# A layer norm's reciprocal root moved from ScalarE's Ln and Exp to VectorE's bit trick and three Newton steps

## The chip, the cores and the metric

One core of one Trainium2 chip runs the whole program in one launch. The metric is device time in microseconds (us), lower is better. The comparison is between the kernel before and the kernel with the change, on the same chip.

## The reference, cut to what matters

The model is one graph layer followed by one mixture-of-experts layer over 12,500 nodes of 256 features and 200,000 edges. Only the front of the graph layer is touched:

```python
def _layernorm(x, axis=-1, eps=1e-05):
    m = jnp.mean(x, axis=axis, keepdims=True)
    v = jnp.var(x, axis=axis, keepdims=True)
    return (x - m) / jnp.sqrt(v + eps)

ft = (feat @ W).reshape(n, H, OUT)            # feat = _layernorm(x), 4 heads of 64
e_src = jnp.sum(ft * w_att_src, axis=-1)      # per node and head
e_dst = jnp.sum(ft * w_att_dst, axis=-1)
e = leaky_relu(e_src[src] + e_dst[dst])       # per edge, softmax over the edges of dst
out = segment_sum(ft[src] * a, dst)           # then x + out, layer norm, experts
```

## The kernel before, in words

The program is a row of stages, each of which is a block that all engines enter and leave together: constants, edge rows, edge tables, **features**, a look-up table of scores, the main stage over the edges, and the experts. The change is in `features` (L720 to L874) and in the two helpers that it calls, `layer_norm_steps` (L92) and `rsqrt_guess` (L121). The main stage calls `rsqrt_guess` too (L1238), for its own layer norm, and that call stays.

`features` works on 98 tiles of 128 nodes, in 14 batches of HB = 7 tiles. Batches alternate between two halves of every buffer (h = 0 for even batches, 1 for odd). For one batch:

- SyncE loads 7 tiles of x in one transfer (L747) and stores 7 rows of results to the table in memory (L754). Its queue is in order. One turn of its loop waits until the even batch's norm is done, loads the next even batch, does the same for the odd batch, and then waits for ScalarE's rows and stores the even batch and the odd batch. So the load of the next even batch stands behind the store of the odd batch before.
- VectorE takes 7 statistics (L98), 7 aggregations (L102), adds epsilon (L104), and then asks ScalarE for a guess of the reciprocal root: `dve.wait_ge(ln_given, nth)`. One Newton step of four small operations follows (L106 to L112), and 7 normalising operations of 128x256 (L117). Those wait until TensorE is through with the batch that used the same buffer before.
- ScalarE computes that guess as Exp(-0.5 * Ln(v)) (L125, L127). In its program the guess for batch q + 1 stands in the middle of batch q, at tile u = 2, after the copy for tile 3 and ahead of the rows of tile 2. Its other work for every tile is a copy of the transposed tile from PSUM (L809), a copy of the result row of 264 values (L822) and of 8 scores (L823).
- TensorE transposes a tile (L844) and multiplies it with the weights (L860); it transposes tile u + 1 ahead of multiplying tile u. The multiplication of tile u waits for ScalarE's copy of u, and for ScalarE's rows of tile u - 2, since there are two result banks.

Each step is ordered by semaphores written out by hand; `Steps.did` and `Steps.settle` put a semaphore wait between any two dependent VectorE operations. At the stage's last batches SyncE's queue is special: the last load has a short tile, for which it waits until VectorE has cleared the buffer after norm 12, and the stores of batches 10 and 11 stand behind that.

Of the kernel before, what the change touches and what calls it, by code (L numbers as in the profile page):

```python
# [7 lines left out]
I32 = mybir.dt.int32  # L8
ALU = mybir.AluOpType
# [4 lines left out]
P = 128  # L14
# [34 lines left out]
HB = 7  # L49
# [4 lines left out]
EPS = 1e-5  # L54
# [9 lines left out]
RSQRT_BITS = float(0x5f3759df)  # L64
# [24 lines left out]
        self.engine.wait_ge(self.sem, self.base + self.n)  # L89

def layer_norm_steps(nc, st, raw, stats, mv, rs, normed, n, ln_asked, ln_given, nth, free=None):  # L92

    dve = nc.vector
    v, r, t = rs
    for i in range(n):
        st.did(dve.bn_stats(stats[:, i, :], raw[:, i, :]))  # L98
    st.settle()
    st.did(dve.memset(t[:, 0:n], 0.0))  # L100
    for i in range(n):
        st.did(dve.bn_aggr(mv[:, i, :], stats[:, i, :]))  # L102
    st.settle()
    dve.tensor_scalar(v[:, 0:n], mv[:, 0:n, 1], EPS, None, ALU.add).then_inc(ln_asked, 1)  # L104
    dve.wait_ge(ln_given, nth)
    st.did(dve.tensor_tensor(t[:, 0:n], r[:, 0:n], r[:, 0:n], ALU.mult))  # L106
    st.settle()
    st.did(dve.tensor_tensor(t[:, 0:n], t[:, 0:n], v[:, 0:n], ALU.mult))
    st.settle()
    st.did(dve.tensor_scalar(t[:, 0:n], t[:, 0:n], -0.5, 1.5, ALU.mult, ALU.add))  # L110
    st.settle()
    st.did(dve.tensor_tensor(t[:, 0:n], t[:, 0:n], r[:, 0:n], ALU.mult))  # L112
    if free is not None:
        dve.wait_ge(*free)
    st.settle()
    for i in range(n):
        st.did(dve.tensor_scalar(normed[:, i, :], raw[:, i, :], mv[:, i, 0:1], t[:, i:i + 1],  # L117
                                 ALU.subtract, ALU.mult))

def rsqrt_guess(nc, n, v, r, asked, given, between, nth):  # L121

    act = nc.scalar
    act.wait_ge(asked, nth)
    act.activation(r[:, 0:n], v[:, 0:n], ACT.Ln).then_inc(between, 1)  # L125
    act.wait_ge(between, nth)
    act.activation(r[:, 0:n], r[:, 0:n], ACT.Exp, scale=-0.5).then_inc(given, 1)  # L127
# [589 lines left out]
def features(nc, x, K, table):  # L717
# [3 lines left out]
    with ExitStack() as ctx:  # L721
        sb = lambda n, s, d=F32: ctx.enter_context(nc.sbuf_tensor("f_" + n, s, d))
        xin = [sb(f"xin{h}", [P, HB, D]) for h in range(2)]
        xn = [sb(f"xn{h}", [P, HB, D]) for h in range(2)]
        rowbuf = [sb(f"rowbuf{h}", [P, HB, ROW]) for h in range(2)]
        xT = [sb(f"xT{i}", [P, 2 * P]) for i in range(2)]
        stats, mv = sb("stats", [P, HB, 6]), sb("mv", [P, HB, 2])
        rs = (sb("v", [P, HB]), sb("r", [P, HB]), sb("t", [P, HB]))
        psT = [ctx.enter_context(nc.psum_tensor(f"f_T{i}", [P, 512], F32)) for i in range(2)]
        psF = [ctx.enter_context(nc.psum_tensor(f"f_F{i}", [P, 512], F32)) for i in range(2)]  # L730
        names = ("padded", "steps", "asked", "given", "between", "normed", "turned", "copied",
                 "multiplied", "row_made", "scored")
        padded, steps, asked, given, between, normed, turned, copied, multiplied, row_made, scored = [
            ctx.enter_context(nc.semaphore("f_" + n)) for n in names]
        loaded = [ctx.enter_context(nc.semaphore(f"f_loaded{h}")) for h in range(2)]
        stored = [ctx.enter_context(nc.semaphore(f"f_stored{h}")) for h in range(2)]
        block = ctx.enter_context(nc.Block("features"))
        LAST = NQ // 2 - 1
        STEPS = 3 * HB + 5

        def rows_of(t, q, n=HB):
            return t[bass.ds(q * (HB * P), n * P), :].rearrange("(b p) d -> p b d", p=P)
# [1 line left out]
        @block.sync  # L744
        def _(sp):
            def load(q, h):
                sp.dma_start(xin[h][:, :, :], rows_of(x, q)).then_inc(loaded[h], 16)  # L747

            def freed(h, it):
                sp.wait_ge(normed, 2 * it + h + 1)  # L750

            def store(q, h, it):
                sp.wait_ge(row_made, (2 * it + h + 1) * HB)
                sp.dma_start(rows_of(table, q), rowbuf[h][:, :, :]).then_inc(stored[h], 16)  # L754

            def iteration(it, more):
                freed(0, it)
                load(2 * it + 2, 0)
                freed(1, it)
                if more:  # L760
                    load(2 * it + 3, 1)
                else:

                    sp.dma_start(xin[1][:, 0:HB - 1, :], rows_of(x, NQ - 1, HB - 1)).then_inc(loaded[1], 16)
                    sp.wait_ge(padded, 1)
                    sp.dma_start(xin[1][0:LASTROWS, HB - 1, :], x[(NB - 1) * P:N, :]).then_inc(loaded[1], 16)
                store(2 * it, 0, it)
                store(2 * it + 1, 1, it)

            load(0, 0)  # L770
            load(1, 1)
            with sp.Fori(0, LAST - 1) as it:
                iteration(it, True)
            iteration(LAST - 1, False)
            store(2 * LAST, 0, LAST)
            store(2 * LAST + 1, 1, LAST)
            for h in range(2):
                sp.wait_ge(stored[h], 16 * (LAST + 1))

        @block.vector  # L780
        def _(dve):
            def norm(q, h, it, first=False, extra=0):
                st = Steps(dve, steps, q * STEPS)
                dve.wait_ge(loaded[h], 16 * (it + 1) + extra)

                layer_norm_steps(nc, st, xin[h], stats, mv, rs, xn[h], HB, asked, given, q + 1,
                                 None if first else (multiplied, (q - 1) * HB))
                st.settle()
                dve.nop().then_inc(normed, 1)
                assert st.n == STEPS  # L790

            nc.vector.memset(K.scores[:, NB:NBD, :], 0.0)
            norm(0, 0, 0, first=True)
            norm(1, 1, 0, first=True)
            with dve.Fori(1, LAST) as it:
                norm(2 * it, 0, it)
                norm(2 * it + 1, 1, it)
            norm(2 * LAST, 0, LAST)
            dve.wait_ge(normed, 2 * LAST)
            nc.vector.memset(xin[1][64:P, HB - 1, :], 0.0).then_inc(padded, 1)  # L800
            norm(2 * LAST + 1, 1, LAST, extra=16)

        @block.scalar
        def _(act):
            def make_rows(q, h, it, more=True):
                def copy_turned(u):
                    k = (h * HB + u) % 2
                    act.wait_ge(turned, q * HB + u + 1)
                    nc.scalar.activation(xT[k][:, :], psT[k][:, 0:2 * P], ACT.Copy).then_inc(copied, 1)  # L809

                copy_turned(0)
                for u in range(HB):
                    i = q * HB + u
                    k = (h * HB + u) % 2
                    if u + 1 < HB:
                        copy_turned(u + 1)
                    if u == 2 and more:
                        rsqrt(q + 1)
                    if u == 0 and it is not None:
                        act.wait_ge(stored[h], 16 * it)  # L820
                    act.wait_ge(multiplied, i + 1)
                    nc.scalar.activation(rowbuf[h][:, u, :], psF[k][:, 0:ROW], ACT.Copy).then_inc(row_made, 1)  # L822
                    nc.scalar.activation(K.scores[:, bass.ds(i, 1), :].rearrange("p a b -> p (a b)"),  # L823
                                         psF[k][:, MSG:NF], ACT.Copy).then_inc(scored, 1)

            rsqrt = lambda q: rsqrt_guess(nc, HB, rs[0], rs[1], asked, given, between, q + 1)
            rsqrt(0)
            make_rows(0, 0, None)
            make_rows(1, 1, None)
            with act.Fori(1, LAST) as it:  # L830
                make_rows(2 * it, 0, it)
                make_rows(2 * it + 1, 1, it)
            make_rows(2 * LAST, 0, LAST)
            make_rows(2 * LAST + 1, 1, LAST, more=False)

        @block.tensor
        def _(pe):
# [1102 lines left out]
```

## Time and profile before

| | us |
|---|---|
| median of 3 runs | 3243.91 (3243.89 to 3252.16) |
| the profiled execution | 3247.97 |
| its span in the profile | 3246.2 |
| mean granted TensorE clock | 0.863 |
| PE, DVE, ACT, POOL busy | 2351.3, 1787.3, 1503.8, 2189.2 |
| feature stage, first x load to last table store's issue | 81.3 to 261 |

The span is the time between the first and the last recorded instruction; the execution's own time has 1.8 us around it. Times of rows count from the span's start. The busy sums cover all stages together, while stages follow one another, so they don't tell what bounds the feature stage; windows and timelines of that stage do.

### The profile page before, as it was taken

The numbers are of one execution on the slowest core, as the hardware profiler recorded it, in microseconds if no ns is written. First come the engines' busy times: TensorE is split into PE (matmuls) and PEld (weight loads), VectorE is DVE, ScalarE is ACT, GpSimd is POOL, SyncE is SP. The second block draws the span as 40 slices with busy tenths as digits, with TensorE's granted clock in tenths as the row PEclk, the third lists the DMA queues.
The fourth block names the chain that finished last, engine by engine and source line by source line (L and its number), as shares of the span: only waits on it lengthen the run. The fifth ranks groups of instructions, "written<-read, shape, count | busy, mean of one in ns | idle before, by whom it ended". The sixth has DMA issues, their size and how long they took to land. (4 is left out here: it accounts for less than half of the span.)

```text
span 3246.2 us, 61769 instructions
## 1 busy us (share of the span) xinstructions
PE 2351.3 (72%) x15568; PEld 1904.9 (59%) x15569; DVE 1787.3 (55%) x3822; ACT 1503.8 (46%) x2731; POOL 2189.2 (67%) x2064
## 2 busy tenths in 40 slices
PE   2673666667667677667777777777767999898995
PEld 1552545555555555556565666666646787777774
DVE  4453444445555556667677777777769433332232
ACT  0562222333344444445555565666654554444442
POOL 0004777777777777777777777777614777777775
PEclk9996777778787777888888888899888999999997
DMA  3444555555555555566666566656524355545443
GB/s 96 146 147 134 155 156 155 157 162 164 165 165 164 166 166 168 167 175 178 173 185 181 173 187 177 182 176 186 164 78 63 62 79 81 81 78 80 80 79 47
DMA packets 232170, 452.82 MB, mean 139 GB/s; under 512 B 55832, under 2 KB 148796, under 8 KB 230783
## 3 DMA queue, kind: packets, MB, share of 16 engines
q0 software_dynamic: 114816, 265.53, 35.2%
q1 hardware_dynamic: 76924, 142.54, 13.7%
q10 hardware_dynamic: 39924, 38.86, 3.7%
q8 instruction: 213, 3.49, 0.4%
q14 instruction: 293, 2.40, 0.2%
HBM read 379.15 MB, written 69.01 MB: 138 GB/s over the span
## 5 line engine op out<-in xcount | busy, mean ns | idle before, releaser
L977 POOL DMA_INDIRECT m_rows<-table,src_col x1568 | 1600.1, 1020 | 729.3 <-issue 700.1
L1363 PE MATMUL m_A<-m_msg,m_by_edge 128*128 128x260 f32 x3920 | 1176.3, 463 | 259.0 <-issue 207.4
L1363 PEld LDWEIGHTS m_A<-m_msg,m_by_edge 128*128 128x128 f32 x3920 | 895.9, 235 | 451.9 <-issue 270.3
L1217 ACT ACTIVATE m_apart<-m_drow,nid 128x1024 bf16 x297 | 341.0, 1148 | 726.2 <-SPq L945 684.9
L1053 DVE TENSOR_TENSOR m_msg<-m_rows,m_A 128x2048 f32<-128x2048 f32 (+1 forms) x294 | 568.2, 1932 | 115.1 <-issue 109.3
L1349 PE MATMUL m_E<-m_look_parts,m_by_node 128*128 x7104 | 246.9, 168 | 259.4 <-ACT m_by_node L1220 258.7
L1349 PEld LDWEIGHTS m_E<-m_look_parts,m_by_node 128*128 128x128 bf16 x7104 | 232.8, 98 | 343.7 <-issue 307.4
L1571 POOL DMA_INDIRECT out<-x_con,x_to_i x206 | 329.2, 1598 | 105.0 <-issue 78.7
L1029 DVE TENSOR_TENSOR m_z<-m_E,m_rows 128x64 f32<-128x64 f32 x295 | 65.9, 224 | 566.9 <-PE m_E L1349 435.7
L1220 ACT ACTIVATE m_by_node<-m_apart,m_one 128x1024 bf16<-128x1024 bf16 x297 | 340.9, 1148 | 9.7
L1013 DVE SCALAR_TENSOR_TENSOR m_by_edge<-dst_col,m_less_base,row 128x1024 f32<-128x1024 f32 (+1 forms) x295 | 325.3, 1103 | 0.7 <-issue 0.2
L1738 DVE TENSOR_TENSOR x_con<-x_X,x_b 128x512 f32<-128x512 f32 x103 | 71.2, 692 | 391.3 <-DMA out<-x_con,x_to_i 358.9
L1562 POOL DMA_INDIRECT x_yr<-ydram,x_from_i x206 | 204.9, 995 | 65.9 <-issue 62.1
L1797 ACT ACTIVATE x_h<-x_H,x_b 128x256 f32<-128x256 f32 x206 | 86.4, 470 | 298.0 <-PE x_H L1852 298.0
L1852 PE MATMUL x_H<-x_yT,x_c 128*128 128x256 f32 x824 | 201.6, 388 | 13.7 <-issue 11.4
L1225 ACT ACTIVATE m_z<-m_z 128x32 f32<-128x32 f32 x295 | 67.3, 228 | 302.7 <-issue 157.5
L1863 PE MATMUL x_X<-x_c,x_h 128*128 128x256 f32 x824 | 195.5, 381 | 2.8 <-DVEq L1745 2.8
L1852 PE MATMUL x_G<-x_h,x_c 128*128 128x256 f32 x824 | 194.7, 379 | 0.0
L1787 ACT ACTIVATE x_c<-x_w 128x512 f32 x309 | 182.7, 627 | 6.0 <-DVEq L1719 5.1
L1852 PEld LDWEIGHTS x_H<-x_yT,x_c 128*128 128x128 f32 x824 | 149.6, 191 | 44.7 <-issue 28.5
L1863 PEld LDWEIGHTS x_X<-x_c,x_h 128*128 128x128 f32 x824 | 157.1, 191 | 24.2 <-issue 3.2
L1852 PEld LDWEIGHTS x_G<-x_h,x_c 128*128 128x128 f32 x824 | 156.9, 190 | 20.9
(245 smaller groups left out, 2232.3 us busy)
## 6 DMA issues: line engine op xcount, KB each, us to landing
m_drow<-edges SPq DMA_DIRECT2D x196, 512.0 KB
m_rows<-table,src_col POOLq DMA_INDIRECT x1568
table<-f_rowbuf SPq DMA_DIRECT2D x14, 924.0 KB, 5.0
ydram<-m_y ACTq DMA_DIRECT2D x49, 264.0 KB
m_xb<-in_x ACTq DMA_DIRECT2D x48, 256.0 KB
out<-m_x ACTq DMA_DIRECT2D x48, 256.0 KB
f_xin<-in_x SPq DMA_DIRECT2D x13, 896.0 KB, 6.5
x_w<-in_L_ffn_expert_w SPq DMA_DIRECT2D x18, 256.0 KB, 5.7
```

The source lines that it names most:

```text
L977: nc.gpsimd.indirect_dma_start(rows[:, g % RING, j, :], None, table, bass.IndirectOffsetOnAxis(ap=K.src_col[:, g, j:j + 1], axis=0)).then_ ...
L1013: v.scalar_tensor_tensor(by_edge[q][:, tiles, :], K.dst_col[:, bass.ds(group, 1), tiles].rearrange("p a j -> p (a j)").unsqueeze(2).broadc ...
L1053: v.tensor_tensor(msg[i][:, tiles, 0:D].rearrange("p j (h n) -> p j h n", h=HEADS), rws[:, tiles, 0:D].rearrange("p j (h n) -> p j h n", h ...
L1217: a.activation(apart[i][:, :], drow[:, bass.ds(g % RING, 1), :].rearrange("p a n -> p (a n)"), ACT.Abs, bias=K.nid[:, bass.ds(b, 1)], scal ...
L1220: a.activation(by_node[i][:, :], apart[i][:, :], ACT.Relu, bias=one[:, 0:1], scale=-1.0)\
L1349: m = t.matmul(psE[i][:, 8 * j:8 * j + 8], by_node[i][:, j * P:(j + 1) * P], look_parts[:, bass.ds(b, 1), 8 * n:8 * n + 8].rearrange("p a ...
L1363: m = t.matmul(psA[i][:, 0:MSG], by_edge[i][:, j, :], msg[i][:, j, :], start=(j == tiles[0]), stop=(j == tiles[-1]))
L1562: g.indirect_dma_start(yr[t % YR][:, i, :], None, ydram, bass.IndirectOffsetOnAxis(ap=from_i[:, 2 * t + i:2 * t + i + 1], axis=0))\
L1571: g.indirect_dma_start(out, bass.IndirectOffsetOnAxis(ap=to_i[:, 2 * t + i:2 * t + i + 1], axis=0), con[t % CR][:, i, :], None, bounds_che ...
L1787: a.activation(into[t % 2][:, :, :].rearrange("p c n -> p (c n)"), of[:, bass.ds(expert(t), 1), :, :].rearrange("p e c n -> p (e c n)"), A ...
L1852: i = t_.matmul(ps[t % 2][:, m * TILE:(m + 1) * TILE], weight[t % 2][:, c, m * P:(m + 1) * P], of[t % 2][:, c, :], start=(c == 0), stop=(c ...
L1863: m = t_.matmul(psX[t % 2][:, i * D:(i + 1) * D], h2[t % 2][:, c, i * P:(i + 1) * P], c3[t % 2][:, c, :], start=(c == 0), stop=(c == 1))
```

## The change

In `layer_norm_steps` the request to ScalarE and the wait for it go. VectorE adds epsilon, shifts the variance's bits right by one as an integer (`arith_shift_right`), computes RSQRT_BITS minus that as the bits of the first guess, and runs three Newton steps of three operations. The normalising operations read the root from `r` and not from `t`. In `features` ScalarE's program no longer holds the guess: it has only its copies. The main stage is as it was.

```diff
-def layer_norm_steps(nc, st, raw, stats, mv, rs, normed, n, ln_asked, ln_given, nth, free=None):
+def layer_norm_steps(nc, st, raw, stats, mv, rs, normed, n, free=None):
...
-    dve.tensor_scalar(v[:, 0:n], mv[:, 0:n, 1], EPS, None, ALU.add).then_inc(ln_asked, 1)
-    dve.wait_ge(ln_given, nth)
-    st.did(dve.tensor_tensor(t[:, 0:n], r[:, 0:n], r[:, 0:n], ALU.mult))
+    st.did(dve.tensor_scalar(v[:, 0:n], mv[:, 0:n, 1], EPS, None, ALU.add))
     st.settle()
-    st.did(dve.tensor_tensor(t[:, 0:n], t[:, 0:n], v[:, 0:n], ALU.mult))
+    st.did(dve.tensor_scalar(half_bits[:, 0:n], v[:, 0:n].bitcast(I32), 1, None, ALU.arith_shift_right))
     st.settle()
-    st.did(dve.tensor_scalar(t[:, 0:n], t[:, 0:n], -0.5, 1.5, ALU.mult, ALU.add))
-    st.settle()
-    st.did(dve.tensor_tensor(t[:, 0:n], t[:, 0:n], r[:, 0:n], ALU.mult))
+    st.did(dve.tensor_scalar(r[:, 0:n].bitcast(I32), half_bits[:, 0:n], -1.0, RSQRT_BITS, ALU.mult, ALU.add))
+    for _ in range(3):
+        st.settle()
+        st.did(dve.tensor_tensor(t[:, 0:n], r[:, 0:n], r[:, 0:n], ALU.mult))
+        st.settle()
+        st.did(dve.scalar_tensor_tensor(t[:, 0:n], t[:, 0:n], -0.5, v[:, 0:n], ALU.mult, ALU.mult))
+        st.settle()
+        st.did(dve.scalar_tensor_tensor(r[:, 0:n], t[:, 0:n], 1.5, r[:, 0:n], ALU.add, ALU.mult))
...
-                    if u == 2 and more:
-                        rsqrt(q + 1)
...
-            rsqrt = lambda q: rsqrt_guess(nc, HB, rs[0], rs[1], asked, given, between, q + 1)
-            rsqrt(0)
```

## Rows read from the trace of the kernel before

**Rows 1.** Windows, one per feature batch: us, busy by engine, PEclk, DMA.
```profile
95.69:108.28 12.59, 10.53 (x42) 8.05 (x43) 6.34 (x28) 7.73 (x23) 0.00 (x0) 1.00 0.22 74
108.28:120.77 12.49, 10.09 (x44) 7.79 (x42) 7.98 (x34) 7.90 (x25) 0.00 (x0) 0.86 0.50 150
120.77:131.74 10.97, 8.37 (x44) 6.58 (x42) 4.11 (x22) 7.91 (x25) 0.00 (x0) 1.00 0.54 170
131.74:144.54 12.80, 10.05 (x44) 7.64 (x42) 8.20 (x34) 7.90 (x25) 0.00 (x0) 0.87 0.50 147
...
155.62:168.19 12.57, 9.93 (x43) 7.60 (x42) 8.07 (x33) 7.90 (x25) 0.00 (x0) 0.87 0.47 148
...
190.30:203.04 12.74, 10.05 (x43) 7.75 (x42) 7.47 (x33) 8.07 (x25) 0.00 (x0) 0.87 0.50 151
...
214.04:226.78 12.74, 10.05 (x44) 7.86 (x43) 7.68 (x33) 8.07 (x25) 0.00 (x0) 0.87 0.52 157
226.78:237.78 11.00, 8.37 (x44) 6.58 (x43) 4.46 (x23) 7.90 (x25) 0.00 (x0) 1.00 0.17 60
237.78:251.38 13.60, 10.03 (x43) 7.58 (x42) 6.20 (x28) 7.80 (x25) 0.00 (x0) 0.87 0.44 146
251.38:260.26 8.88, 8.27 (x43) 6.41 (x41) 0.00 (x0) 5.15 (x21) 0.00 (x0) 1.00 0.31 107
```

**Rows 2.** Timeline, TensorE and ScalarE: start, us, engine, what, [idle before it <-releaser].
```profile
153.81 1.97 PE L860 MATMUL f_F<-wcat,f_xT 128*128 128x268 f32 x8
155.62 0.60 PE L844 MATMUL f_T<-ident,f_xn 128*128 128x128 f32 x4
...
159.90 1.28 ACT L125 ACT_TABLE_LOAD   x1
161.42 1.28 ACT L127 ACT_TABLE_LOAD   x1
162.83 0.37 ACT L822 ACTIVATE f_rowbuf<-f_F 128x264 f32<-128x264 f32 x1
163.59 1.17 PE L860 MATMUL f_F<-wcat,f_xT 128*128 128x268 f32 x4 [2.02 <-ACT f_xT L809]
```

**Rows 3.** Timeline, VectorE in one batch, with the next batch's first operation.
```profile
155.62 2.39 DVE L98 BATCH_NORM_STATS2 f_stats<-f_xin 128x6 f32<-128x256 f32 x7 [0.51 <-DVE f_xn L117]
158.66 0.17 DVE L104 TENSOR_SCALAR f_v<-f_mv 128x7 f32<-128x7 f32 x1
162.96 0.17 DVE L106 TENSOR_TENSOR f_t<-f_r 128x7 f32<-128x7 f32 x1 [4.13 <-ACT f_r L127]
163.76 2.35 DVE L117 TENSOR_SCALAR f_xn<-f_xin,f_mv,f_t 128x256 f32<-128x256 f32 x7
166.26 2.39 DVE L98 BATCH_NORM_STATS2 f_stats<-f_xin 128x6 f32<-128x256 f32 x7
```

**Rows 4.** Groups of instructions by line and shape, other stages: busy us, mean ns.
```profile
L1113 DVE SCALAR_TENSOR_TENSOR m_newton<-m_newton,m_var 128x2 f32<-128x2 f32 x49 | 7.9, 162 | 1.7
L1669 DVE TENSOR_SCALAR x_rest_i<-x_rest_i 128x6 int32<-128x6 int32 x1 | 0.2, 171 | 0.0
```

**Rows 5.** Timeline, SyncE's queue and ScalarE's wait at batch 12.
```profile
192.02 0.40 SPq L747 DMA_DIRECT2D f_xin<-in_x  x1
...
243.27 0.39 ACT L822 ACTIVATE f_rowbuf<-f_F 128x264 f32<-128x264 f32 x1 [4.28 <-DMA table<-f_rowbuf]
```

**Rows 6.** The page, transfers: KB each, median us from issue to landing.
```profile
f_xin<-in_x SPq DMA_DIRECT2D x13, 896.0 KB, 6.5
```

**Rows 7.** Timeline, the stage after the features, its first operation.
```profile
265.82 0.85 DVE L634 TENSOR_REDUCE lt_ends<-scores 128x4 f32<-128x392 f32 x1 [14.88 <-PEq L721]
```

**Rows 8.** Groups of ScalarE's instructions by line, whole span.
```profile
L125 ACT ACT_TABLE_LOAD x63 | 80.8, 1283 | 86.4 <-PEq L428 81.2 <-issue 2.5
...
L1228 ACT ACTIVATE m_msg<-m_z 128x32 f32<-128x32 f32 x295 | 67.6, 229 | 9.4
```

**Rows 9.** The page's first line.
```profile
span 3246.2 us, 61769 instructions
```

More of the change, by code:

```diff
@@ L89, in settle @@
         self.engine.wait_ge(self.sem, self.base + self.n)
-def layer_norm_steps(nc, st, raw, stats, mv, rs, normed, n, ln_asked, ln_given, nth, free=None):
+def layer_norm_steps(nc, st, raw, stats, mv, rs, normed, n, free=None):
     dve = nc.vector
-    v, r, t = rs
+    v, r, t, half_bits = rs
     for i in range(n):
@@ L116, in layer_norm_steps @@
     for i in range(n):
-        st.did(dve.tensor_scalar(normed[:, i, :], raw[:, i, :], mv[:, i, 0:1], t[:, i:i + 1],
+        st.did(dve.tensor_scalar(normed[:, i, :], raw[:, i, :], mv[:, i, 0:1], r[:, i:i + 1],
                                  ALU.subtract, ALU.mult))
@@ L727, in features @@
         stats, mv = sb("stats", [P, HB, 6]), sb("mv", [P, HB, 2])
-        rs = (sb("v", [P, HB]), sb("r", [P, HB]), sb("t", [P, HB]))
+        rs = (sb("v", [P, HB]), sb("r", [P, HB]), sb("t", [P, HB]), sb("half_bits", [P, HB], I32))
         psT = [ctx.enter_context(nc.psum_tensor(f"f_T{i}", [P, 512], F32)) for i in range(2)]
         psF = [ctx.enter_context(nc.psum_tensor(f"f_F{i}", [P, 512], F32)) for i in range(2)]
-        names = ("padded", "steps", "asked", "given", "between", "normed", "turned", "copied",
-                 "multiplied", "row_made", "scored")
-        padded, steps, asked, given, between, normed, turned, copied, multiplied, row_made, scored = [
+        names = ("padded", "steps", "normed", "turned", "copied", "multiplied", "row_made", "scored")
+        padded, steps, normed, turned, copied, multiplied, row_made, scored = [
             ctx.enter_context(nc.semaphore("f_" + n)) for n in names]
@@ L738, in features @@
         LAST = NQ // 2 - 1
-        STEPS = 3 * HB + 5
+        STEPS = 3 * HB + 13
         def rows_of(t, q, n=HB):
@@ L784, in norm @@
                 dve.wait_ge(loaded[h], 16 * (it + 1) + extra)
-                layer_norm_steps(nc, st, xin[h], stats, mv, rs, xn[h], HB, asked, given, q + 1,
+                layer_norm_steps(nc, st, xin[h], stats, mv, rs, xn[h], HB,
                                  None if first else (multiplied, (q - 1) * HB))
@@ L804, in _, with make_rows @@
         def _(act):
-            def make_rows(q, h, it, more=True):
+            def make_rows(q, h, it):
                 def copy_turned(u):
@@ L833, in _ @@
             make_rows(2 * LAST, 0, LAST)
-            make_rows(2 * LAST + 1, 1, LAST, more=False)
+            make_rows(2 * LAST + 1, 1, LAST)
         @block.tensor
```

## The prediction

> **What bounds the kernel now.** I read the page first and then left it: its busy sums run over stages that follow one another, and the span of 3246.2 us [rows 9] is worth something here only as the ruler. The question is what sets the length of the feature stage, and whether its end sets the rest. The second is quickly read: the next stage's first operation comes at 265.82, after VectorE has idled for 14.88 us, released by the end of the block [rows 7]. Every microsecond taken off the end of the features moves all later stages up by the same.
>
> The first I read from windows cut at TensorE's first transposition of every batch [rows 1]. The 14 batches take 95.69 to 260.26, 164.57 us, and fall into four kinds. Six take 10.97 to 11.11 at full clock (two of them are shown). Five take 12.49, 12.80, 12.57, 12.74 and 12.74 with a mean granted clock of 0.86 or 0.87. Two are special, batch 0 (12.59) and batch 12 (13.60). The last, batch 13, takes 8.88 to the end of its last matmul. It is the only batch in which ScalarE computes no guess for a next one, so it is a measurement of the stage without what the change removes. To compare it with the others, which are cut where the next transposition starts: that start lies 0.16 us ahead of the end of the matmuls before it (153.81 + 1.97 = 155.78 against 155.62) [rows 2]. So a batch without guess takes 8.88 - 0.16 = 8.72 us, and one with guess 11.00, of which TensorE is busy 8.37.
>
> Where the 2.28 us go stands in the timeline of one batch. ScalarE loads a table at 159.90, another at 161.42, and gets to the rows of tile 2 at 162.83. That is 2.93 us in which it copies nothing, and TensorE's next matmul at 163.59 has idled 2.02 us for ScalarE's copy of a transposed tile [rows 2]. VectorE meanwhile waits 4.13 us for the guess [rows 3], but it is not late: its wait costs nothing as long as the normed tiles come before TensorE ends the batch. So TensorE, held up by ScalarE's in-order program, is the path, with VectorE and the transfers beside it.
>
> **The change part by part.**
>
> *ScalarE's guess goes.* In 13 batches (0 to 12) the gap in ScalarE's program closes. In the eleven ordinary ones and batch 0 the price is 11.00 - 8.72 = 2.28 us each [rows 1]. In batch 12 ScalarE waits 4.28 us for a store at its first row [rows 5], and the guess partly lies beside the catching-up that follows. What that batch can give lies between 0 and 13.60 - 8.72 = 4.88. The store stands behind norm 12 in SyncE's queue, and norm 12 will come somewhat earlier against TensorE, which takes part of the stall away. I take 2.28 here too, near the middle. Sum: 13 x 2.28 = 29.6 us.
>
> *The clock.* Five batches are longer by (12.49 + 12.80 + 12.57 + 12.74 + 12.74) - 5 x 11.00 = 8.3 us together. They show TensorE's granted clock at the lower of its two levels (1.2 of 2.4 GHz) for part of the batch; in finer windows the fall comes each time one or two microseconds after the idle time of 2.02 us. Batch 13, without that idle time, has 1.00 throughout [rows 1]. With the stall gone I expect none of the five falls: 8.3 us, with 0 as the other end if the short gaps at batch borders were enough. I take the whole, since no fall in this stage lies anywhere but behind a stall. Batch 0's excess over 11.00 (1.59) comes from the start, at the lower level, and stays.
>
> *VectorE's chain in batch 0.* Nothing hides the root there: TensorE waits for the first normed tiles. Before, from the epsilon operation on: that operation (0.20 to the next start), then Ln, one table load and Exp, 162.96 - (159.90 + 1.28) = 1.78, then four small operations from 162.96 to 163.76, 0.80 [rows 2, 3], in all 2.78. (Ln's own table load came before the wait.) After: epsilon, shift, subtraction and nine Newton operations, 12 x 0.20 = 2.40. The nearest rows for the new kinds are an int32 TENSOR_SCALAR of 128x6 at 171 ns and a SCALAR_TENSOR_TENSOR of 128x2 at 162 ns [rows 4], no dearer than the 0.17 of the small ones here. Gain 0.4; between 1.0 and a loss of 0.9 if the steps were 0.15 or 0.31 us.
>
> *VectorE's chain elsewhere.* Per batch: statistics and aggregation 158.66 - 155.62 = 3.04, 2.40 for the root, and from the first normalising operation to the next batch's statistics 2.50 (163.76 to 166.26), or 2.86 at a turn of the loop (0.51 of idle time as at 155.62) [rows 3]. That is 7.94 or 8.30, mean 8.12, against TensorE's 8.72. It is hidden, with only 0.60 us per batch to spare; if the cover is gone each 0.05 us on a small operation costs 0.60 us per batch, and from there on 14 x what is over.
>
> *SyncE and the transfers.* Nothing is issued anew, but the same 1.8 MB per batch must pass in 8.72 us instead of 11.0. The DMA share was 0.54 in such batches [rows 1], so 0.54 x 11.0 / 8.72 = 0.68 now. The tight spot is the load of an even batch behind an odd store: it starts at 192.02 where batch T began at 190.30, so at T + 1.72, lands 6.5 later (median [rows 6]), and needs 3.04 + 2.40 + 2.50 on VectorE: T + 16.2. TensorE asks for it two batches after T, at T + 17.4. Slack 1.2 us per pair; hidden, but next in line.
>
> Sum: 29.6 + 8.3 + 0.4 = 38.3 us. The profiled execution of 3247.97 would become 3209.7; it lay 4.06 above the median of the runs, so against that median 3243.91 - 38.3 = 3205.6. As a check: 14 x 8.72 + 1.59 for batch 0 + 2.6 left for batch 12 = 126.3, 164.57 - 126.3 = 38.3.
>
> *The skill against the trace.* The trace has two loads of 1.28 us per guess and ScalarE's next function right behind each [rows 2]. The Trainium skill, "ScalarE: Activation LUTs", section "Table sets: the hidden batching unit", says that Ln and Exp share a set, so that a sequence of both needs one load; if so here, there would be no loads after the first and a guess would hardly stall TensorE. The trace disagrees: 63 loads stand at L125 [rows 8], one per guess, and one more ahead of each Exp [rows 2]. The same page, "What ACT_TABLE_LOAD costs", gives 2.66 us for a switch with its drain; 13 batches would then give an estimated 13 x 2 x (2.66 - 1.28) = 36 us more. The gap of 2.93 us from the first load to the next copy leaves no room for that, and the measurement decides.
>
> **The rivals.**
>
> *A. The clock still falls.* All else as forecast, but the clock falls in as many batches: gain 30.0, 3213.9. For it: short idle times of TensorE remain at each batch border (0.6 us). Against: they are there in batch 13 too, at 1.00.
>
> *B. VectorE or the even load becomes the bound.* The slacks are 0.60 and 1.2/2 us per batch. If small operations step at 0.26 instead of 0.20, VectorE needs 8.84; if the load lands in 9.2 rather than 6.5 because a load, a store and the next load now overlap more, a pair is 1.5 us late. Six pairs x 1.5 = 9 us given back: 3214.6. For it: the chain is really close. Against: bandwidth is there (share 0.68).
>
> *C. Slower: table loads move into the main stage.* ScalarE's Exp for the edges (L1228, 295 times) finds its table without any load: the main stage's loads all stand at L125 and L127. At the stage's entry that rests on the feature stage having ended with Exp's table. Afterwards the features hold only copies. If the placement then puts a load ahead of Exp in every item, that is 295 x 1.283 = 378 us of ScalarE [rows 8], up to 3243.9 - 38.3 + 378 = 3584 if all of it were on the path. The change turns slower once over 38.3 / 1.283 = 30 of the 295 loads are exposed; a quarter exposed gives 3300. Against: the last guess of each pair leaves Exp's table behind, so one load at the entry is enough, 1.3 us at most.
>
> *D. The change doesn't pay:* the shorter features are given back in a later stage, within 10 us of before. Nothing in [rows 7] speaks for it: the next stage waits for the block.
>
> **How the numbers follow.** Forecast 0.66 (3205.6, own range 3200 to 3210), A 0.10, B 0.15, C 0.03, D 0.03, and a gain above 46 us 0.03. The range 3198 to 3217 holds the forecast, A and B and leaves out C, D and the tails. This measurement tells apart changes above 0.3%, 9.7 us. Faster by more takes in the forecast, A, B, the larger gain: 0.94. Within: D, 0.03. Slower: C, 0.03.
>
> **What would show it.** Right: batches 1 to 11 at 8.7 us from transposition to transposition, a granted clock of 1.00 from batch 1 to 11, no idle time of about 2 us ahead of L860, no table load between 96 and 222 us, VectorE idle for short times only, and a stage end near 222 instead of 260; later stages as long as before. Wrong: batches of 9.5 us or more with TensorE's transposition released by the norm (B), falls of the clock (A), more than 50 table loads at the main stage or any ahead of L1228 beyond the first (C), or small VectorE operations that start more than 0.25 us apart.

## The result: 24.7 us faster, 13.6 us less than forecast

The changed kernel takes 3219.31 us (median of 4 runs, 3216.11 to 3222.28), the kernel before 3244.01 us beside it (median of 4, 3243.89 to 3252.16): ratio 0.9918, 95% interval 0.9898 to 0.9937. The sign is as forecast; the size is not: 3205.6 was predicted, with a range of 3198 to 3217. Two more samples of the same kernel, below, gave 26.9 and 23.7 us.

The profiled execution took 3221.51 us, with this first line of the page:

```profile
span 3219.8 us, 61872 instructions
```

The span is 26.4 us shorter than the 3246.2 of [rows 9]. First the features, cut at TensorE's first transposition of each batch as in [rows 1] (us, busy by engine in the order PE, PEld, DVE, ACT, POOL, granted clock, DMA share, GB/s):

```profile
95.01:105.25 10.24, 10.19 (x42) 7.99 (x43) 9.40 (x41) 4.98 (x19) 0.00 (x0) 0.79 0.36 102
105.25:113.77 8.52, 8.13 (x43) 6.54 (x42) 7.82 (x39) 5.16 (x21) 0.00 (x0) 1.00 0.62 205
113.77:122.46 8.69, 8.11 (x44) 6.54 (x42) 5.15 (x27) 5.15 (x21) 0.00 (x0) 1.00 0.83 263
...
148.69:157.54 8.85, 8.11 (x44) 6.55 (x43) 6.54 (x33) 5.26 (x21) 0.00 (x0) 1.00 0.76 233
...
192.57:201.24 8.67, 8.10 (x43) 6.54 (x42) 7.09 (x34) 5.15 (x21) 0.00 (x0) 1.00 0.25 82
201.24:211.32 10.08, 8.36 (x43) 6.57 (x42) 7.31 (x34) 5.05 (x21) 0.00 (x0) 1.00 0.58 196
211.32:220.16 8.84, 8.27 (x43) 6.41 (x41) 0.00 (x0) 5.15 (x21) 0.00 (x0) 1.00 0.31 107
```

Batches 1 to 11 take 8.52 to 8.89 us where they took 10.97 to 12.80, and the granted clock is 1.00 in each. The last batch, which had no guess before either, is as long as it was (8.84 against 8.88). The stage ends at 220.16 instead of 260.26: 40.1 us earlier. So the features gave what was forecast and 1.8 us more.

The timeline of one batch (start, us, engine, line, what, [idle before it <- releaser]) answers to [rows 2] and [rows 3]:

```profile
150.03 1.14 PE L858 MATMUL f_F<-wcat,f_xT 128*128 128x268 f32 x4 [0.74 <-ACT f_xT L811]
150.32 0.17 DVE L104 TENSOR_SCALAR f_v<-f_mv 128x7 f32<-128x7 f32 x1
150.53 0.17 DVE L106 TENSOR_SCALAR f_half_bits<-f_v 128x7 int32<-128x7 int32 x1
150.73 0.17 DVE L108 TENSOR_SCALAR f_r<-f_half_bits 128x7 int32<-128x7 int32 x1
150.94 0.17 DVE L111 TENSOR_TENSOR f_t<-f_r 128x7 f32<-128x7 f32 x1
...
152.74 2.35 DVE L120 TENSOR_SCALAR f_xn<-f_xin,f_mv,f_r 128x256 f32<-128x256 f32 x7
...
156.91 1.41 DVE L98 BATCH_NORM_STATS2 f_stats<-f_xin 128x6 f32<-128x256 f32 x4 [1.82 <-DMA f_xin<-in_x]
```

TensorE's idle time of 2.02 us is gone; the 0.74 at the head of this batch is all that is left. VectorE's twelve small operations start 0.20 us apart (150.32 to 152.74 is 2.42). VectorE waits for the next load six times, 3.1 us at most, which TensorE doesn't feel.

Then the later stages. The first operation of the next stage [rows 7] is still 40.09 us early:

```profile
225.73 0.85 DVE L637 TENSOR_REDUCE lt_ends<-scores 128x4 f32<-128x392 f32 x1 [15.56 <-PEq L724]
```

The main stage is bracketed by its first and last gather, here of the kernel before and of the changed one (ns min/median/max, first and last start):

```profile
L977 POOL DMA_INDIRECT m_rows<-table,src_col x1568: 947/953/2015, 275.6 to 2372.1; - x196
```

```profile
L975 POOL DMA_INDIRECT m_rows<-table,src_col x1568: 951/957/2016, 235.5 to 2336.5; - x196
```

40.1 us ahead at the first gather, 35.6 at the last. The next loss stands in VectorE's timeline of the experts' routing, first before the change, then after it:

```profile
2442.08 0.26 DVE L1635 TENSOR_TENSOR x_g<-x_top 128x98 f32<-128x98 f32 x1
2442.49 0.77 DVE L1597 TENSOR_TENSOR x_eq<-x_pr,x_top 128x588 f32<-128x588 f32 x1
2443.30 0.77 DVE L1599 TENSOR_TENSOR x_eq<-x_eq,x_rev 128x588 f32<-128x588 f32 x1
...
2447.67 0.26 DVE L1648 TENSOR_TENSOR x_g<-x_g 128x98 f32<-128x98 f32 x1
```

```profile
2407.61 0.26 DVE L1633 TENSOR_TENSOR x_g<-x_top 128x98 f32<-128x98 f32 x1
2408.02 0.77 DVE L1595 TENSOR_TENSOR x_eq<-x_pr,x_top 128x588 f32<-128x588 f32 x1
2413.96 0.77 DVE L1597 TENSOR_TENSOR x_eq<-x_eq,x_rev 128x588 f32<-128x588 f32 x1 [5.17 <-issue]
...
2418.34 0.26 DVE L1646 TENSOR_TENSOR x_g<-x_g 128x98 f32<-128x98 f32 x1
```

34.5 us ahead at the first x_g, 29.3 at the second. Between two operations that followed each other at once, VectorE now stands still for 5.17 us, and "issue" says that no semaphore, no engine and no transfer of the kernel's released it. The stage's code is the same in both kernels. The transfers of that stretch (2405 to 2430) show what else was moved: two packets on the queue of instruction fetches, first the changed kernel, then the same stretch of the kernel before, which has none, and where the kernel's own queue has the whole:

```profile
q1 hardware_dynamic: 13558, 3.38, 81.0%
q14 instruction: 2, 0.02, 0.2%
```

```profile
q1 hardware_dynamic: 12757, 3.13, 100.4%
```

The first of the two begins inside the stop: asked in narrow windows, none lies in 2408.8 to 2412.0 and one in 2412.0 to 2412.4. VectorE stops at 2408.79 and goes on at 2413.96, 1.9 us after that packet began.

So 4.5 us in the main stage, 1.1 between it and the routing, 5.1 in the routing and 2.9 in the experts' part are given back, and the gain of 40.1 becomes 26.4. What these have in common, and which of them is more than the difference between one execution and another, is what the experiments ask. What the change leaves behind for the later stages is where their code stands. Compiled, VectorE's program has 3384 instructions against 3328, since the root is written out once for each call of the norm: 56 more ahead of the main stage, and everything later stands 56 places further down. ScalarE's program is 25 instructions shorter (3024 against 3049); the other engines' are as long as before.

### The profile page after: what moved, and what is told of

Same layout as the page of the kernel before. It is cut to its first block and busy times, and to the rows that moved or that the text cites. A ratio compares the mean times of both kernels' runs of the same rounds, so it can differ in the third digit from the quotient of the medians.

```text
span 3219.8 us, 61872 instructions
## 1 busy us (share of the span) xinstructions
PE 2336.7 (73%) x15568; PEld 1893.7 (59%) x15569; DVE 1801.8 (56%) x3920; ACT 1465.8 (46%) x2676; POOL 2197.1 (68%) x2064
```

## The experiments

Theory P (place): the features give 38 to 40 us; the rest is lost because VectorE's later code stands 56 instructions further down, so that the fetching of the program falls elsewhere. Rival N (noise): the profiles of after and before differ in the main stage by chance, and the gain is smaller for a reason inside the features. Rival V: VectorE became the bound.

Runs of one kernel scatter: before ran 16 times in the first comparison, 3233.75 to 3250.25. So medians with their intervals count, and a single profile tells a millisecond-long stage only to about 5 us.

### The changed kernel again: again, again3

No edit.

> The changed kernel once more, for a second profile and a tighter time. In the first profile the feature stage ends 40.1 us earlier than before, and 13.6 us of that are gone by the end: VectorE idles 5.2 us in the experts' routing for no semaphore while a fetch of instructions lands, and the main stage and the experts lose 8.5 us bit by bit. Theory (the losses come from where the longer VectorE program is cut into instruction fetches): the same idle time stands at the same line again, in most executions, and the time lies 3216 to 3223. Rival (noise of one execution): the idle time is gone and the saving is near 38 us, 3206.

> The changed kernel itself, for the comparison on this chip: gain 23 to 30 us, idle time of 5 us in the routing. R and M agree.

Measured: 3215.71 (ratio 0.9917, interval 0.9896 to 0.9938), 26.9 us below before; and 3219.54 (0.9928, 0.9914 to 0.9942), 23.7 below. The idle time ahead of x_eq is there each time, and always 5.2 or 5.3. The 4.5 us of the main stage are not: from first to last gather these two took 2090.3 and 2089.9 us, where the first profile showed 2101.0 and the kernel before 2096.5. What came again is the gain of 24 to 27 us and the idle time, and each time a packet of instructions begins inside it, 1.9 us before VectorE goes on (at 2400.8 in again, at 2401.7 in again3).

### The guess without tables, on ScalarE: linear_guess

The kernel before, its Ln and Exp replaced by two functions that load no table. The guess is good only where the variance is near 1, as the rows here have it; the Newton step behind it stays.

```diff
-            rsqrt = lambda q: rsqrt_guess(nc, HB, rs[0], rs[1], asked, given, between, q + 1)
+            rsqrt = lambda q: linear_guess(nc, HB, rs[0], rs[1], near_one, asked, given, between, q + 1)
...
+    act.activation(r[:, 0:n], v[:, 0:n], ACT.Copy).then_inc(between, 1)
+    act.wait_ge(between, nth)
+    act.activation(r[:, 0:n], r[:, 0:n], ACT.Relu, bias=bias[:, 0:1], scale=-0.5).then_inc(given, 1)
```

> The kernel before with the features' guess as two ScalarE functions that need no table load: a copy of v and Relu(1.5 - 0.5 v), which is the root's tangent at v = 1 (the norm is then approximate, within a few 1e-4 for these inputs). VectorE's program stays as it was, but for one memset. Theory (the two table loads of 1.28 us are what holds TensorE up, and later stages lose only where VectorE's program is longer): the feature stage is 35 to 40 us shorter, later stages as before, 3204 to 3209. Rival 1 (the wait between the engines holds the stage, not the loads): the stage gains less than 15 us, above 3229. Rival 2 (the later losses come with the earlier end of the features): 3216 to 3223.

Measured: 3204.83 (0.9882, 0.9859 to 0.9904), 37.8 us below before. ScalarE's program in the middle of a batch:

```profile
152.99 0.39 ACT L821 ACTIVATE f_xT<-f_T 128x256 f32<-128x256 f32 x1
153.25 0.22 ACT L134 ACTIVATE f_r<-f_v 128x7 f32<-128x7 f32 x1
153.50 0.30 ACT L136 ACTIVATE f_r<-f_r,f_near_one 128x7 f32<-128x7 f32 x1
153.56 0.38 PE L857 MATMUL f_T<-ident,f_xn 128*128 128x128 f32 x2
153.76 0.39 ACT L834 ACTIVATE f_rowbuf<-f_F 128x264 f32<-128x264 f32 x1
```

The guess is still on ScalarE, with its wait and its semaphores, but takes 0.5 us instead of 2.93, and TensorE doesn't stop for it. That settles the cause in the features: the loads, not the round trip, held TensorE. It does more. This kernel's gathers start at 238.7, 3 us later than the changed kernel's, and yet the whole is 11 us faster. Its VectorE program is one instruction longer than before, not 56, and the routing shows no idle time. The later stages lose nothing here, against N, which has no reason for the difference.

### The program longer, nothing else: before_pad56

```diff
             norm(2 * LAST + 1, 1, LAST, extra=16)
+            for i in range(56):
+                nc.vector.memset(pads[:, i:i + 1], 0.0)
```

> The kernel before with 56 memsets of one element per partition on VectorE after its last norm, where VectorE waits 15 us for the others: as many instructions as the change adds to VectorE's program. 56 x 0.06 = 3.4 us lie inside that wait. Theory (place of the instructions in the fetches): an idle time of some 5 us in the experts' routing appears, as in the changed kernel, and the time rises by 5 us or more, to 3249 or above. Rival (the losses come from the earlier phase or the new arithmetic, not from the length of the program): 3244, no idle time there.

Measured: 3253.0 (9 runs; 1.0034, 1.0022 to 1.0046), 10.4 us above before. The idle time of VectorE in the routing (waited for: total, times, longest) is the changed kernel's, at the same operation:

```profile
DVE x_eq L1602 <- issue: 5.3, 1, 5.3
```

The memsets themselves lie where VectorE waits for the block to end; the first gather even starts 0.8 us earlier than before's. So 56 instructions that compute nothing cost what the changed kernel was missing, but for 1 to 3 us. P holds, and V isn't needed. ScalarE's program is here as long as before, so its shorter program in the changed kernel isn't needed either.

### The changed kernel, moved further: after_pad200, after_pad72, after_pad12

The same loop of memsets behind the last norm, with 200, 72 and 12 columns. Everything later stands 256, 128 and 68 places further down than before the change.

> The changed kernel with 200 memsets of one element per partition on VectorE after its last norm, 200 x 0.06 = 12.8 us inside the 15.6 us that VectorE waits there. 56 + 200 = 256 instructions are 16 KB more than before. 
> The changed kernel with 12 memsets on VectorE after its last norm. In the changed kernel the idle time of 5.2 us stands ahead of the operation of L1597's second pass, the 1946th of VectorE's program. Theory (a fixed place in the program's memory at which a new piece must be fetched): the idle time is now 12 instructions earlier in the program, ahead of the reciprocal (L1622 of the changed kernel), where the weights are being loaded as well; 3212 to 3222. Rival (that line waits for something of its own): it stays at L1597.

Measured: 3204.6 with 200 (0.9872, 0.985 to 0.9894; 38.0 us below before), 3200.85 with 72 (0.9875, 0.9844 to 0.9907; 39.7 below), 3208.55 with 12 (0.989, 0.986 to 0.992; 32.0 below). With 200 and 72 the routing has no idle time; with 12:

```profile
DVE x_tot L1625 <- issue: 3.0, 1, 3.0
```

This is another operation, twelve instructions ahead of x_eq, and so the same place in the program: in both kernels the stop lies at VectorE's instruction 1946, counted from 0. It is bound to the place and not to what is computed there, as P says; here it is 3.0 us long instead of 5.2. With 72 another short stop appears, 2.9 us at the end of the main stage, behind its loop (m_sums, at 2360.85), and costs nothing that can be seen. Adding 200 useless instructions makes the changed kernel 11 us faster than again in the same series: the forecast of 38.3 us is what these two kernels give. All three were faster than their expectations said (3204.6 against 3211 to 3214, 3200.85 against 3205 to 3211, 3208.55 against 3212 to 3222): the routing's stop isn't all that the place costs.

### Less traffic beside the fetch: late_weights

```diff
             k = lambda t: t.rearrange("e (c p) n -> p e c n", p=P)
+            sp.wait_ge(sel_made, 1)
```

SyncE loads the experts' weights only when the routing's selection is there.

> The changed kernel, in which SyncE waits for the selection (sel_made, behind the second pass of L1597) before it loads the experts' weights. Theory (the fetch queues behind 18 weight loads of 256 KB that keep the transfer engines 90% busy): the fetch comes in time or costs under 2 us, the idle time at L1597 goes, and the time falls by 3 to 6 us against the changed kernel's 3215.7; the weights are wanted only 100 us later. Rival (the fetch is slow whatever else is moved): the idle time of 5 us stays.

Measured: 3215.22 (0.991, 0.9882 to 0.9939), 25.3 below before; not told apart from again. The stop is shorter:

```profile
2409.14 0.77 DVE L1598 TENSOR_TENSOR x_eq<-x_eq,x_rev 128x588 f32<-128x588 f32 x1 [1.99 <-issue]
```

1.99 instead of 5.17: taking the kernel's own transfers out of the way takes 3.2 us off a stop that no semaphore of the kernel explains. The packet of instructions shows where they went. It begins 0.2 us into this stop and 3.3 us into that of the first profile, and from its start VectorE needs 1.8 us here and 1.9 there. That makes the stop a fetch of the program which queues behind the kernel's transfers, 2.0 us by itself.

The expected 3 to 6 us didn't show. In the trace another stop has grown beside the moved transfers: ScalarE stands still for 8.9 us ahead of x_off (L1765), released by nothing, where the changed kernel has 1.9 at that place, and TensorE waits 7.2 us for it. A packet of instructions lies inside that one too, amid the small packets of the transfers.

### How close VectorE is: newton6_pad128

```diff
-    for _ in range(3):
+    for _ in range(6):
```

Nine more small operations per batch, and 128 memsets so that the later stages stand 256 places further down, as in after_pad200.

> The changed kernel with six Newton steps in place of three, and 128 memsets after the last norm, so that with the 72 instructions of the added steps and the 56 of the change the later stages stand as with 200 memsets (3204.6). Nine more operations x 0.20 = 1.8 us per batch make VectorE's cycle 9.74 or 10.10 us against TensorE's 8.72. Theory (VectorE had 0.60 us per batch to spare): the feature stage gets 12 x (9.92 - 8.72) = 14 to 18 us longer, TensorE's first transposition of a batch waits for the norm, 3219 to 3223. Rival (VectorE far from the path): under 5 us more.

Measured: 3221.61 (0.9933, 0.991 to 0.9956), 17.0 us more than after_pad200. TensorE's waits for the norm in the features (the first is the start):

```profile
PE f_T L845 <- DVEq L792: 31.4, 9, 22.2
```

Eight waits of (31.4 - 22.2) / 8 = 1.15 us. The forecast had VectorE at 8.12 us per batch against TensorE's 8.72; nine more at 0.20 make 9.92, 1.20 over. Batches 3 to 10 took 10.07 us on average, so without the nine VectorE would need about 8.3 (an estimate, 10.07 - 9 x 0.20) where a batch of the changed kernel takes 8.73. The slack was real, 0.5 us rather than 0.6, and V is refuted: without these nine, VectorE isn't the bound. after_pad200 ran in another series; by the differences to before it is 19.1 us (38.0 - 18.9), by after_pad72 of the same series 20.8.

### Which of the later stages: again2, pad72_again, main_end_pad72, pad200_main_end56

In this series every run took a quarter longer (before: 4042.93, 29 runs, 4025.21 to 4075.32), and the intervals are plus or minus 10 to 13 us. The 800 us more lie between the first and the last gather (2899.5 us in again2, 2090.3 in again), and there VectorE waits 890 us in again2 for something that the profile only calls remote, a wait that again doesn't have. What it is, no run tells; these differences are no measure for the other series. The new edit puts memsets behind the main stage's loop, so that the routing moves and the loop stays:

```diff
                     normalize(dve.snap(pair, min_val=0, max_val=NPAIR - 1))
+            for i in range(72):
+                v.memset(end_pads[:, i:i + 1], 0.0)
```

> The changed kernel for the third time, on the same chip as the next three. Both theories: 26 to 28 us faster than before, idle time of 5.2 us at L1597.

> The changed kernel with 72 memsets after the last norm once more: 38 to 41 us faster than before, no idle time in the routing. It is the comparison for the next two, which pad other stages apart.

> The changed kernel with 72 memsets at the end of VectorE's main-stage program, where it waits 9 us for the others. The main stage's instructions stand as in the changed kernel, the experts' as with 72 memsets after the features, so the routing has no idle time. Theory 1 (the whole loss lies in the routing): as fast as pad72_again, 38 to 41 us under before. Theory 2 (the loss over the 5.2 us comes from the main loop, where the changed kernel has a short idle time once in each of the 14 turns of the loop ahead of an operation that ScalarE waits for): 31 to 34 us under before.

> The changed kernel with 200 memsets after the last norm, which puts the main stage's instructions where they stood before, and 56 at the end of the main stage, which puts the experts' where the change put them. The routing's idle time of 5 us is back at L1597. Theory 1 (the whole loss lies in the routing): as slow as the changed kernel, 26 to 28 us under before. Theory 2 (part of it lies in the main loop): 33 to 36 us under before.

Measured, below before: again2 22.2 us (0.9937, 0.991 to 0.9964), main_end_pad72 26.8 (0.9939, 0.9913 to 0.9966), pad200_main_end56 29.9 (0.9923, 0.9899 to 0.9947), pad72_again 36.5 (0.9915, 0.9882 to 0.9948). The order is as in the other series, but the intervals overlap: inconclusive, and main_end_pad72's median lies below what either of its theories had. One thing is clear: main_end_pad72 has no idle time in the routing, nor has pad200_main_end56, which was built to bring it back (it was also one instruction off, 313 places instead of 312).

### One stage moved at a time: before_end55, before_pad56_end71, main_end_pad71

The same two edits, on the kernel before and on the changed one, now counted to the instruction (the memsets at the loop's end bring one instruction of their own), in a series where before ran 23 times at 3243.25.

> The kernel before with 55 one-column memsets at the end of VectorE's part of the main stage. Everything behind the main stage stands 56 instructions later in VectorE's program (as in the changed kernel), the loop of the main stage stands where it did. Theory R (the routing's idle time of 5 us and what follows from it is the whole of the lost gain): the idle time of 5 us stands ahead of the second pass of x_eq, and the time is as much above before as with 56 memsets behind the norms, +7 to +12 us (55 memsets themselves are 3 us of VectorE at most, behind the last item). Theory M (the place of the main stage's loop in the program costs the other half): the idle time stands there too, but the time is only +4 to +7 us.

> The kernel before with 56 memsets behind the norms and 71 more at the end of VectorE's part of the main stage: the main stage's loop stands 56 instructions later, what is behind it 128. Theory R: no idle time in the routing, time within 3 us of before. Theory M: no idle time in the routing either, but +4 to +8 us, all of it in the main stage (first to last gather about 5 us longer than before's).

> The changed kernel with 71 memsets at the end of VectorE's part of the main stage; main stage's loop as in the changed kernel, routing moved by 128 in all. No idle time of 5 us in the routing. Theory R: the gain against before is 36 to 42 us. Theory M: 29 to 34 us.

| kernel | main stage moved by | routing moved by | against before, us | idle in routing |
|---|---|---|---|---|
| before_end55 | 0 | 56 | +2.2 (1.0009, 0.9998 to 1.0019) | none |
| before_pad56_end71 | 56 | 128 | +6.7 (1.0018, 1.0007 to 1.0029) | none |
| before_pad56 | 56 | 56 | +10.4 (1.0034, 1.0022 to 1.0046) | 5.3 |
| main_end_pad71 | 56 | 128 | -28.9 (0.9909, 0.9889 to 0.993) | none |
| again, again3, first result | 56 | 56 | -26.9, -23.7, -24.7 | 5.2 to 5.3 |
| after_pad12 | 68 | 68 | -32.0 (0.989, 0.986 to 0.992) | 3.0 |
| after_pad72, after_pad200 | 128, 256 | 128, 256 | -39.7, -38.0 | none |

Two things follow. The main stage's place very likely costs something by itself: before_pad56_end71 has no idle time in the routing and is slower than before by 2.3 to 9.4 us. The memsets at the loop's end are not the reason in its trace: the last of them is over at 2425.9, ScalarE issues transfers until 2427.4 and the next stage begins at 2428.9. They also move some of the main stage's buffers in memory by up to 288 bytes; before_end55, with 224 and the loop in its old place, is above before by 2.2 us (-0.6 to 6.2), so a part of the 6.7 may be theirs. On the changed kernel the same step is the 9 to 11 us between main_end_pad71 and the last row, which is from other series, with intervals that overlap a little. The idle time in the routing costs the rest, 10.4 - 6.7 = 3.7 on one side and 28.9 - 25.1 (the mean of the three) = 3.8 on the other, each a difference of medians that are good to 3 us at best.

The traces say much the same: from x_earlier, the next stage's first VectorE operation, to the end takes 816.8 to 818.8 us with the loop at its old place or 128 or 256 further and no stop in the routing (six profiles), 820.4 and 821.1 with the loop moved by 56 and no stop, 823.4 to 828.1 with the stop (four). So 2 to 3 us of what goes with the loop's place are spent behind the main stage.

The expectation for before_end55 missed: the routing stands there at the changed kernel's place (x_eq is VectorE's instruction 1946 in both), and the stop is absent. Both theories of that expectation had the stop there, and both were wrong in it. The packets of instructions show more. With the loop at its old place (before, before_end55, linear_guess) or moved by 128 or 256 (after_pad72, after_pad200), three of them come at the end of the main stage, and then none for at least 30 us, the routing among them. With the loop moved by 56 or 68 only two come there, and the third comes later, inside a stop: at instruction 1946 in the routing (after, again, again3, before_pad56, after_pad12), or in the memsets (before_pad56_end71, main_end_pad71, which stop there for 2.9 and 2.7 us, without harm since VectorE then waits for GpSimd anyway). before_end55 pays its 2.6 us at m_sums behind the loop. So the stop wasn't gone but moved to where it costs less.

The loop itself fetches more, too. This is the queue's line of the page, over the whole span, of the kernel before and of the changed one:

```profile
q14 instruction: 293, 2.40, 0.2%
```

```profile
q14 instruction: 307, 2.51, 0.3%
```

14 packets more, and the main stage's loop has 14 turns. All kernels with the loop moved by 56 or 68 have 307 or 308, all others 293 to 296, those of the 4000 us series too. One more fetch of 8 KB in each turn is thus what goes with the slower layouts. That it costs the 7 to 10 us is argued, not shown.

VectorE's waits show the loop's place as well. Of those for nothing named, the kernel before has the first of these lines, and all seven profiles of the 3200 us series with the loop moved by 56 have the second in its stead (here of before and after); after_pad12, after_pad72, after_pad200, newton6_pad128 and before_end55 have the first, linear_guess neither:

```profile
DVE m_A L1046 <- issue: 3.7, 9, 0.4
```

```profile
DVE m_z L1031 <- issue: 3.4, 14, 0.3
```

Stops of 0.4 us ahead of m_A, nine of them, have become stops of a quarter of a microsecond ahead of m_z, fourteen of them; ScalarE waits for m_z before its exponential. The sum is the same, 3.4 against 3.7. The time of the main stage doesn't settle it: from the first to the last gather the profiles with the loop at 56 average 2094.7 (2089.9 to 2101.0, seven), those with it elsewhere 2090.8 (2084.2 to 2096.5, seven), a difference of the right sign but no larger than their scatter. before_pad56_end71, expected about 5 us above before there, took 2095.1 against 2096.5.

## Why the prediction missed

Step by step, by the forecast's own terms.

*The step that failed* is in its first paragraph: "Every microsecond taken off the end of the features moves all later stages up by the same." That was read off [rows 7], which shows only that the next stage waits for this one. It does move up (40.09 us), but the later stages then took 13.7 us longer, 40.1 - 26.4. The experiments give that loss a cause in 10 to 14 us of it: 56 instructions more in VectorE's program, some 4 us of it with the stop in the routing, 5.2 us long, and 7 to 10 with the place of the main stage's loop. The split rests on differences of medians whose intervals overlap; the sum doesn't, before_pad56 shows it at 7 to 15 us. Nothing in the forecast counted instructions; the change was costed by what they do. Rival D ("given back in a later stage", 0.03) named the right direction, but a loss to within 10 us of before and no mechanism.

*ScalarE's guess, 29.6 us:* right. Batches at full clock fell from 11.00 to 8.52 to 8.89, (201.24 - 105.25) / 11 = 8.73 on average where 8.72 was forecast. Batch 12 gave 13.60 - 10.08 = 3.5 where 2.28 was taken: its wait for the store fell from 4.28 to 2.80 us, as the text foresaw, and its granted clock, 0.87 in [rows 1], is 1.00 now, which the forecast's term for the clock left out. linear_guess shows that the loads were the stall.

*The clock, 8.3 us:* right. Before, five ordinary batches had a granted clock of 0.86 or 0.87 behind an idle time of 2.02 us; now TensorE's longest idle time in an ordinary batch is 0.78 us, and the clock is 1.00 from batch 1 on. Rival A is dead.

*Batch 0, 0.4 us:* the start came 0.68 us earlier (95.01 against 95.69), and the batch itself took 10.24, where the forecast left 1.59 over 8.72, 10.31. The forecast put that excess down to the lower level of the clock, though [rows 1] give this batch 1.00. The changed kernel's row gives 0.79, and the first four transpositions take 1.12 us in both profiles, against 0.60 in later batches at 1.00, so it is the 1.00 of that row that is in doubt and not the lower level. In all: 0.68 for the start, 12.59 - 10.24 = 2.35 in batch 0, 129.50 - 95.99 = 33.5 in batches 1 to 11, 3.5 in batch 12 and 0.04 in batch 13 make the 40.1.

*VectorE's cover:* right, to 0.15 us per batch (10.07 measured in newton6_pad128, 9.92 by the forecast's terms). *The transfers:* right; the DMA share of batches 3 to 10 is 0.66 on average where 0.68 was forecast. Rival B is dead. The even load was late for VectorE (1.82 us in the batch shown) and not for TensorE.

*The table loads of the main stage:* they stay one per guess, 49 and 49, at L128 and L130, and Exp of the edges finds its table; rival C is dead. The Trainium skill, "ScalarE: Activation LUTs", section "Table sets: the hidden batching unit", has Ln and Exp share a set; this trace again has a load ahead of each of them:

```profile
L128 ACT ACT_TABLE_LOAD x49 | 62.9, 1283 | 3.9 <-issue 1.2
L130 ACT ACT_TABLE_LOAD x49 | 62.9, 1283 | 0.9
```

Had the two shared a set here, linear_guess would have had almost nothing to win, and it won 37.8 us.

*The median:* 3205.6 needed the loss to be zero. It is zero in after_pad72 (3200.85 with before at 3240.51) and after_pad200 (3204.6 with before at 3242.6), and there the sum of 38.3 is met: 39.7 and 38.0. These are the versions to take: the change with its later code moved to another place. linear_guess equals them without it, for inputs of variance near 1 only.

*What stays open:* whether the one more fetch in each turn of the loop is what its place costs, and why the part behind the main stage takes 2 to 3 us longer with it.

## What to carry to other kernels

Count the instructions that a change adds to an engine's program, not only their time, and after it look through all later stages for idle time released by nothing: here 56 cheap, hidden instructions took a third of a gain of 38 us, and 72 useless ones gave it back. Look at the queue of instruction fetches beside such a stop, and count its packets over the span. To tell such a loss from the change's own effect, build the old kernel with as many empty instructions and nothing else. And where an engine's in-order program feeds another engine, a table load in it is paid by both: 2.56 us of loads cost 2.28 us of TensorE per batch, and 1.7 more where the clock fell behind it (8.3 over five batches).

## What the runs showed of the hardware

- VectorE stops with no semaphore behind it while a packet of its program is fetched: 5.2 or 5.3 us at one instruction for one layout, 3.0 at another operation in the same place for the next, 2.0 where the transfers of that time are moved away. It goes on 1.8 to 2.0 us after the packet begins; the rest is the packet's delay, 3.3 to 3.4 us (after_pad12: 1.2) while the experts' transfers run and 0.2 without them.
- Which layout has the stop in the routing isn't told by the instruction's number alone: number 1946 stops after the loop moved by 56, and doesn't where only the code behind the loop moved. There three packets come at the loop's end instead of two, and a stop of 2.6 us stands behind the loop.
- Moving the loop by 56 or 68 instructions adds about 14 packets of instructions to the span (307 or 308 against 293 to 296; the loop has 14 turns). That this costs time is not shown.
- ScalarE has such stops too: 8.9 us ahead of x_off in late_weights, 1.9 in the changed kernel.
- An int32 shift and an int32 subtraction of 128x7 in VectorE take 171 ns and start 0.20 to 0.21 us apart, as the float operations of that size do.
- The kernel before took 3240.5 to 3244.0 us in four series of runs and 4042.9 in one, with the ratio of the two kernels nearly unchanged (0.9918 and 0.9937).
